# Three of four weight slots of a mixture of experts filled during the graph convolution ahead of it, in memory that its tables leave

## What is computed

```python
x = x + L0_gnn(layernorm(x), edges, edge_weight, ...)   # adapter, then two graph convolutions
x = x + L0_ffn(layernorm(x), ln_w, w_router, wi, wo)    # 16 experts, one per token
x = x + L1_gnn(...)                                     # two graph attention layers
x = x + L1_ffn(...)                                     # attention with three gated experts

def L0_ffn(x, ln_w, w_router, wi, wo):                  # wi: 16 x 768 x 384, wo: 16 x 384 x 768
    normed = x * rsqrt(mean(x * x) + 1e-6) * ln_w
    expert = argmax(softmax(normed @ w_router))         # at most 64 tokens each
    h = relu(normed[tokens of e] @ wi[e])
    return x + prob * (h @ wo[e])                       # scattered back to the tokens
```

## Time and profile before

| what | value |
|---|---|
| runs | 1711.87, 1712.66, 1713.43 us (median 1712.66) |
| the profiled execution | 1712.41 us, its span 1711.2 us |
| granted TensorE clock, mean | 0.93 of full speed |
| PE busy | 1432.6 us (84% of the span) |
| DVE, ACT, POOL busy | 1016.9, 551.6, 208.0 us |
| moved by DMA | 102.47 MB, mean 60 GB/s |

### The profile page before, as it was taken

The page is one execution under the profiler, slowest core; times in us unless marked ns, Lnnn a source line. Parts: engine busy times, 40 slices in busy tenths (PEclk is TensorE's granted clock), DMA queues, the critical chain, the costliest instruction groups (busy, mean ns, idle before and its releaser), DMA issues. The chain is left out here.

```text
span 1711.2 us, 24706 instructions
## 1 busy us (share of the span) xinstructions
PE 1432.6 (84%) x8462; PEld 1107.7 (65%) x8463; DVE 1016.9 (59%) x1869; ACT 551.6 (32%) x1271; POOL 208.0 (12%) x324
## 2 busy tenths in 40 slices
PE   4898988999287479718888869999889999999997
PEld 3577776856143245417787845555568898898987
DVE  7588886267411459989999945612236452363254
ACT  2588880004310251115555531300022231231122
POOL 0122220400020000000000022000046103102100
PEclk8899998999589669959999989999989999999999
DMA  5000001021899713101212021000021001000011
GB/s 154 1 0 0 0 0 47 1 83 29 311 324 392 240 47 86 46 1 30 60 31 60 1 80 30 1 0 0 0 67 47 19 1 47 29 1 28 10 46 46
DMA packets 78374, 102.47 MB, mean 60 GB/s; under 512 B 33898, under 2 KB 58599, under 8 KB 77167
## 3 DMA queue, kind: packets, MB, share of 16 engines
q1 hardware_dynamic: 76242, 93.14, 18.0%
q0 software_dynamic: 1280, 6.29, 1.0%
q10 hardware_dynamic: 770, 1.92, 0.4%
HBM read 90.33 MB, written 11.01 MB: 59 GB/s over the span
## 5 line engine op out<-in xcount | busy, mean ns | idle before, releaser
L1517 PE MATMUL ps<-B,gat_room 125*125 125x97 f32 x1600 | 196.3, 279 | 76.1 <-DVE gat_room L1477 76.1
L1517 PEld LDWEIGHTS ps<-B,gat_room 125*125 125x125 f32 x1600 | 183.7, 191 | 89.1 <-DVE gat_room L1477 86.7
L513 PE MATMUL ps<-gat_room,g_A 125*128 125x250 bf16 x1600 | 182.7, 272 | 21.7 <-ACT g_A L547 21.7
L513 PEld LDWEIGHTS ps<-gat_room,g_A 125*128 125x128 bf16 x1600 | 153.0, 98 | 46.1 <-ACT g_A L547 29.7
L1270 DVE CUSTOM_DVE_ANT_0 g_junk<-g_srow,MN 125x1250 bf16<-125x1250 f32 x90 | 138.7, 1541 | 21.5 <-DMA g_srow<-ald 15.0
L547 ACT ACTIVATE g_A<-g_A,g_act_edges 125x128 bf16<-125x128 bf16 x400 | 127.7, 390 | 41.2 <-DVE g_A L472 41.2
L1472 ACT ACTIVATE gat_room<-gat_room,g_scol 125x1250 f32<-125x1250 f32 x80 | 106.9, 1338 | 103.7 <-DVE gat_room L1466 103.7
L1466 DVE SCALAR_TENSOR_TENSOR gat_room<-g_ab,g_scol 125x1250 f32<-125x1250 f32 x80 | 120.4, 1506 | 2.8 <-PE ps L1517 2.3
L1477 DVE SCALAR_TENSOR_TENSOR gat_room<-gat_room,CT 125x1250 f32<-125x1250 f32 x80 | 116.1, 1451 | 1.3 <-ACT gat_room L1472 1.3
L1459 PE MATMUL ps<-gat_room,A 128*125 128x384 f32 x240 | 80.2, 498 | 0.0
L1459 PE MATMUL ps<-gat_room,B 128*125 128x384 f32 x240 | 79.4, 495 | 0.0
(11 more groups left out here) (364 smaller groups left out, 2860.5 us busy)
## 6 DMA issues: line engine op xcount, KB each, us to landing
expert_w<-in_L_ffn_wi_dram SPq DMA_DIRECT2D x10, 1152.0 KB, 12.2
g_ab<-abd SPq DMA_DIRECT2D x9, 1093.8 KB
arena<-in_L_ffn_wo_dram SPq DMA_DIRECT2D x8, 1152.0 KB, 14.5
gat_room<-in_L_ffn_wi_dram SPq DMA_DIRECT2D x6, 1152.0 KB, 16.2
expert_w<-in_L_ffn_wo_dram SPq DMA_DIRECT2D x6, 1152.0 KB, 13.8
g_srow<-ald SPq DMA_DIRECT2D x9, 546.9 KB
c_fold_w<-in_L_gnn_W_dram SPq DMA_DIRECT2D x12, 384.0 KB, 5.1
gat_room<-in_L_gnn_W_dram SPq DMA_DIRECT2D x4, 1152.0 KB, 12.1
```

The lines of the kernel that those rows point to most:

```text
L513: last = nc.tensor.matmul(sums[:, off:off + T * WIN], A[:, h, i, g, :], G[:, h, g, :], start=False, stop=True, skip_group_check=True)
L1517: last = nc.tensor.matmul(ps[:NT, bank, at:at + C + 1], P[:, i % PR, t * NT:(t + 1) * NT], hx[:, s, h, :], start=(s == 0 and t % GO == 0), ...
```

## The change

The ring is made before the first block. Slots 0 and 1 become two tensors of their own, `expert_w0` and `expert_w1`. The tables of `dense_graph` are carved out of slot 0 and the inputs of the convolution out of slot 1, as far as they fit; a tile that does not fit stays a tensor. `carve` rounds each piece to 8 words of 4 bytes. The fold buffers `fold_w` and `prod` and DVE's `tmp` move into the part of `A` behind `hw2`, so their first transfers have to wait until PE has read `XT` for the last time (`hw_done`).

SP then loads pair 0 at the start of `gcn`, pair 1 after the fourth slice of the fold (by then the inputs in slot 1 are used up), and pair 2 at the end of `gcn`, when PE has read the matrix in `arena` for the last time. `route` loads only pair 3, and `b1` goes behind the rows. As the code stands, pair 3 is issued ahead of the rows, not behind them.

```diff
+def carve(nc, c, slot, prefix):
+    taken = [0]
+    def sb(name, shape, dt=F32):
+        words = -(-math.prod(shape[1:]) * (2 if dt in (BF16, I16) else 4) // 32) * 8
+        if taken[0] + words > slot.shape[1]:
+            return c.enter_context(nc.sbuf_tensor(prefix + name, shape, dt))
+        flat = slot[:shape[0], taken[0]:taken[0] + words]
+        taken[0] += words
...
-def graph_inputs(nc, c, room):
+def graph_inputs(nc, c, room, slot):
-    sb = lambda n, shape, dt=F32: c.enter_context(nc.sbuf_tensor(n, shape, dt))
+    sb = carve(nc, c, slot, "")
...
-def edge_tables(nc, c, low):
+def edge_tables(nc, c, low, slot):
+    sb = carve(nc, c, slot, "g_")
+    A = sb("A", [EPC, 2, 4, HALF_GR, 128], BF16)
...
 def gcn(...):
-        fold_w, prod = sb("fold_w", [128, FR, D]), sb("prod", [128, 2, D])
-        tmp = sb("tmp", [NT, 2, H])
+        f0 = T * H
+        fold_w = room[:, f0:f0 + FR * D].rearrange("p (i n) -> p i n", i=FR)
+        prod = room[:, f0 + FR * D:f0 + (FR + 2) * D].rearrange("p (i n) -> p i n", i=2)
+        tmp = room[:NT, f0 + (FR + 2) * D:f0 + (FR + 2) * D + 2 * H].rearrange("p (i h) -> p i h", i=2)
...
         def _(sp):
+            load_pair(sp, ins, ring, 0)
+            sp.wait_ge(hw_done, T)
             for layer in range(2):
...
                     sp.dma_start(fold_w[:, j % FR, :], ...).then_inc(fold_in[j % FR], 16)
+                    if j == FR:
+                        load_pair(sp, ins, ring, 1)
...
                 sp.dma_start(moe["lnw"][p0:p1], ...).then_inc(moe["lnw_in"], 16)
+            sp.wait_ge(aggT_done, 6)
+            load_pair(sp, ins, ring, 2)
...
 def route(...):
-            for j in range(SLOTS):
-                load_pair(sp, ins, ring, j)
-            sp.dma_start(g["b1"][:], ...).then_inc(g["b1_in"], 16)
+            load_pair(sp, ins, ring, 3)
             for t in range(0, T, 2):
                 sp.wait_ge(scaled, t + 2)
                 for p0, p1 in ROWS:
                     sp.dma_start(normd[...], XN[p0:p1, t:t + 2, :]).then_inc(stored, 16)
+            sp.dma_start(g["b1"][:], ...).then_inc(g["b1_in"], 16)
             sp.wait_ge(stored, LANDED * T // 2)
...
 def program(...):
+                slots = [early.enter_context(nc.sbuf_tensor(f"expert_w{i}", [128, 2 * K * FF], F32)) for i in range(2)]
+                ring = expert_ring(nc, early, slots + [arena[:, T * D:T * D + 2 * K * FF], g["room"][:, 0:2 * K * FF]])
...
-                    low = graph_inputs(nc, dense, g["room"])
+                    low = graph_inputs(nc, dense, g["room"], slots[1])
-                    tab = edge_tables(nc, tables, low)
+                    tab = edge_tables(nc, tables, low, slots[0])
```

More of the change, by code:

```diff
@@ L169 @@
 H_GCN = 256
-def graph_inputs(nc, c, room):
-    sb = lambda n, shape, dt=F32: c.enter_context(nc.sbuf_tensor(n, shape, dt))
+def carve(nc, c, slot, prefix):
[6 more added lines that the diff above has]
+        taken[0] += words
+        flat = (flat if dt == F32 else flat.bitcast(dt))[:, 0:math.prod(shape[1:])]
+        names = "abcd"[:len(shape) - 1]
+        return flat.rearrange(f"p ({' '.join(names)}) -> p {' '.join(names)}", **dict(zip(names, shape[1:]))) if len(names) > 1 else flat
+    return sb
+def graph_inputs(nc, c, room, slot):
+    sb = carve(nc, c, slot, "")
     g = {"wd": sb("c_wd", [128, K, R]), "wu": sb("c_wu", [R, D]), "bd": sb("c_bd", [96, 1]), "bu": sb("c_bu", [128, K]),
@@ L208 @@
 PACK = 512
-def edge_tables(nc, c, low):
-    def sb(name, shape, dt=F32):
-        return c.enter_context(nc.sbuf_tensor("g_" + name, shape, dt))
-    tab = {"dstf": sb("dstf", [EROWS, EG, EPC]), "srcf": sb("srcf", [EROWS, EG, EPC]), "hi": sb("hi", [EROWS, 2, EG, EPC]),
+def edge_tables(nc, c, low, slot):
+    sb = carve(nc, c, slot, "g_")
+    A = sb("A", [EPC, 2, 4, HALF_GR, 128], BF16)
+    tab = {"A": A, "edge": sb("edge", [EPC, 5, NC_E + GR]), "dstf": sb("dstf", [EROWS, EG, EPC]), "srcf": sb("srcf", [EROWS, EG, EPC]), "hi": sb("hi", [EROWS, 2, EG, EPC]),
            "dlim": sb("dlim", [EROWS, 2, EG]), "lo_iota": sb("lo_iota", [EPC, 128], I16), "key_iota": sb("key_iota", [EPC, T, WIN], I16),
            "win_start": sb("win_start", [EPC, NWIN]), "chunk_no": sb("chunk_no", [EROWS, EG]), "zero_b": sb("zero_b", [EPC, 512], BF16),
-           "edge": sb("edge", [EPC, 5, NC_E + GR]), "wrest": sb("wrest", [EPC, NC_E]), "wb": sb("wb", [EPC, NC_E], BF16),
+           "wrest": sb("wrest", [EPC, NC_E]), "wb": sb("wb", [EPC, NC_E], BF16),
            "meets": sb("meets", [EROWS, EG, NWIN]), "part": sb("part", [EROWS, EG, NWIN]), "marks": sb("marks", [EROWS, 2, EG, NWIN]),
@@ L383, in dense_graph @@
         act_edges = sb("act_edges", [EPC, GR])
-        A = sb("A", [EPC, 2, 4, HALF_GR, 128], BF16)
+        A = tab["A"]
         G = low["spare"][:EPC, 0:GR * T * WIN // 2].bitcast(BF16).rearrange("p (r g n) -> p r g n", r=2, g=HALF_GR)
@@ L568, in _, with gcn @@
             copy_out(NWIN - 1, 6)
-def gcn(nc, ins, low, XT, MT, X, W, stat, ones, ps, g, early, XN, eps_col, moe):
+def gcn(nc, ins, low, XT, MT, X, W, stat, ones, ps, g, early, XN, eps_col, moe, ring):
     H = H_GCN
@@ L800, in expert_ring @@
 def expert_ring(nc, c, rooms):
-    own = c.enter_context(nc.sbuf_tensor("expert_w", [128, SLOTS - len(rooms), 2, K * FF], F32))
-    ring = {"w": [own[:, i, :, :] for i in range(SLOTS - len(rooms))] + [r.rearrange("p (i f) -> p i f", i=2) for r in rooms],
+    ring = {"w": [r.rearrange("p (i f) -> p i f", i=2) for r in rooms],
             "in": [new_sem(nc, c, f"expert_in{i}") for i in range(SLOTS)]}
@@ L862, in _ @@
         def _(sp):
-            for j in range(SLOTS):
-                load_pair(sp, ins, ring, j)
-            sp.dma_start(g["b1"][:], ins["L1_gnn_b1"].rearrange("(k p) -> p k", p=128), allow_slow_non_contiguous=True).then_inc(g["b1_in"], 16)
+            load_pair(sp, ins, ring, 3)
             for t in range(0, T, 2):
@@ L869, in _ @@
                     sp.dma_start(normd[0:N, :].rearrange("(t p) d -> p t d", p=NT)[p0:p1, t:t + 2, :], XN[p0:p1, t:t + 2, :]).then_inc(stored, 16)
+            sp.dma_start(g["b1"][:], ins["L1_gnn_b1"].rearrange("(k p) -> p k", p=128), allow_slow_non_contiguous=True).then_inc(g["b1_in"], 16)
             sp.wait_ge(stored, LANDED * T // 2)
@@ L2375, in program @@
                     tables.close()
-                    gcn(nc, ins, low, XT, MT, X, cst, stat, ones, ps, g, measured[0], XN, eps[:NT, 0:1], moe)
+                    gcn(nc, ins, low, XT, MT, X, cst, stat, ones, ps, g, measured[0], XN, eps[:NT, 0:1], moe, ring)
                 with ExitStack() as s:
-                    ring = expert_ring(nc, s, [arena[:, T * D:T * D + 2 * K * FF], g["room"][:, 0:2 * K * FF]])
                     route(nc, ins, cst, X, XN, XT, stat, eps[:NT, 1:2], moe, ps, normd, ring, g)
```

## The result

| | before | after |
|---|---|---|
| median of 6 runs beside each other, us | 1712.26 (1709.71 to 1714.69) | 1698.92 (1693.86 to 1704.10) |
| ratio, 95% interval | 1 | 0.9918 [0.9899, 0.9936] |
| profiled execution / its span, us | 1712.41 / 1711.2 | 1699.51 / 1698.3 |

What follows compares the result with a forecast made beforehand. The prediction took the transfer queue ahead of the rows in `route` to bound the kernel, with `experts` DMA-bound behind it. -18.6 + 0.3 = -18.3 us from 1712.41 gave 1694.1 us, range 1692.2 to 1699.0.

Steps and rivals of the forecast that it cites:

- What bounds the kernel: In `route`, some 19 us are only a queue of transfers ahead of the gather; DVE's last list is late next.
- Six transfers leave the queue: In `route`, 6.20 MB instead of 13.28 MB at 375 GB/s: rows land at 451.3, gather starts 18.6 us earlier.
- lower bound of 333 GB/s: In `route`, the whole block's mean rate: rows would land at 453.4, leaving a gain of 16.8 us.
- `b1` behind the rows: In `route`, b1 issued after the rows, at about 444 with 9 us until the gathers: taken at 0.
- The fourth pair holds up the rows: Rival in `route`: at 333 GB/s the rows come 1.8 us after DVE's list, giving 1695.9 us; chance 0.18.
- `gcn`: Early loads in `gcn`: pair 0 at 0, pair 1 at 0.3 us, pair 2 at 0; block ends at 429.6 as before.
- Pair 0 and pair 2: At the start and end of `gcn`: price 0 each, pair 0 with 37 us of cover, pair 2 at most 1.05 us.
- Pair 1 ahead of the fifth slice: In `gcn`, fifth slice in place at 365.5, wanted by DVE at 365.55: taken at 0.3 us.
- `experts`: In `experts`, the DMA-bound weight stream moves as a whole with the earlier gather, its rate staying at 385 GB/s.
- no fold was late: Rival in `gcn`: the fifth slice comes late for DVE, 8.7 us lost, giving 1702.5 us; chance 0.09.
- late instruction fetch: Rival in `gcn`: an engine waits 12.8 us for code fetched behind the weight loads, giving 1706.6 us; chance 0.03.
- the one-hot tables kept their rate: Rival in `dense_graph`: DVE's one-hot passes slow to the plain rate, 72 us would show, giving 1766 us; chance 0.03.

Runs made afterwards that it cites:

- the first profile: The changed kernel with no further edit, its first profiled execution: 1699.51 us, ratio 0.9918 against the kernel before.
- the 16 turns: Against the kernel with rows ahead of pair 3 and b1 in `experts`: PE turns the identity 16 times into an unread bank while awaiting the gather; ratio 0.9861.

## Why the prediction was right or wrong

*What bounds the kernel: right.* With the loads back in `route` and all else changed, the time of before returns (1.0006). The queue ahead of the rows is the whole effect, and DVE's list is what is late next, as forecast: with the rows out of the way the gather starts 1.12 us after it.

*Six transfers leave the queue: right in bytes, wrong in rate, and this is the term that was mis-sized.* The sum took 375 GB/s for "2 x 1152 KB and the rows", from a window in which weights were loaded through a full queue. The rows now go out as they are scaled, right behind one pair: the queue moved 298 GB/s from 440 to 454 in the first profile, and rows alone 291 to 300. So they landed 21.2 to 22.3 us after route's first issue and not 19.2, and the gather came 4.1 to 4.5 us after the list and not 1.3. That is 2.8 to 3.2 of the missing us; the rest in the first profile is its longer stream in `experts` and its later start. The lower bound of 333 GB/s, which the prediction set aside, gives 21.3 us and so the near end of what the runs showed. The Trainium skill ("DMA: Bandwidth & Descriptors", Specifications) gives a core some 358 GB/s of device memory; by it, as the prediction estimated, the rows would have come half a us behind DVE's list. Here loads ran at 385, rows out of a full queue at 371 to 407 and rows alone at 291 to 300 GB/s, so no one figure fits, and the measurement decides.

*`b1` behind the rows: taken at 0, and no cost beyond the spread is shown.* The reason given, "I take 0, as it is issued at about 444 and has 9 us until the gathers", did not hold: b1 was issued at 447.73, while the last rows were still in the queue. But without it the rows landed 21.3 us after `route`'s first issue, within the 21.2 to 22.3 with it.

*The fourth pair holds up the rows: the rival that came true.* It was priced at 1.8 us after DVE's list and given 0.18. The rows landed 2.8 to 3.2 us after the list: as late from `route`'s first issue as the rival had them or up to 1 us later, and in two of three profiles the list came 1.1 us earlier. With the rows ahead of the pair the gather comes 1.12 us after the list and not 4.1 to 4.5, with b1 still behind them. So the order of the rows and the pair decides over these 3 us. Why the rows are slow behind a short queue stays open. That the measured time fell inside the range is owed to the room that the range left for this rival and the next, and by 0.1 us only.

*`gcn`: right.* Pair 0 and pair 2 cost nothing (DVE waits 3.43 us for `lnw`, 3.60 before). Pair 1 ahead of the fifth slice was taken at 0.3 us and cost 0; "in place at 365.5, wanted at 365.55" came out as 366.0 and 366.46. What the forecast did not weigh is that the other place that was tried is dearer, because `lnw` is late then.

*`experts`: right.* The stream moves as a whole. The first profile alone shows it 2.4 us longer, the next two do not.

*The rivals that did not come:* no fold was late; from SP's first issue in `gcn` to DVE's list it is 188.4 to 190.9 us in the ten profiles with pair 1 in its place, 190.9 before, which leaves no room for the 12.8 us of a late instruction fetch; and the one-hot tables kept their rate (1.0006 with the same layout).

## What to carry to other kernels

When transfers are taken out from ahead of others in a queue, price what is left at the rate it will have when it goes out by itself, as it becomes ready, not at the rate of the full queue it came out of; and send what somebody waits for ahead of what nobody needs yet. When an edit is worth less than the spread of the runs, measure it as a distance between two events inside the profile, and use the time of the runs only to confirm it. Check first that the event counted from does not itself move from run to run, and repeat the profile before a difference of 1 us is given a cause. A load placed where it just fits can still be well placed: try a neighbouring place before moving it for good.

## What the runs showed of the hardware that was not expected

- The same row packets of 3 KB took 127 ns in the mean behind a full queue (371 GB/s over ten us) and 152 ns in a queue of their own with no engine computing (296 GB/s over ten us); with PE, DVE and ACT computing and nothing ahead it was 151 ns.
- TensorE's granted clock went up to 2.4 GHz within 1 us behind the 16 turns and was down to 1.2 again at 461, PE having had 2.43 us of nothing and then little work; the product that it was meant for ran at the half clock for most of its time.
